# First scores ahead of the setup work: a two-network graph attention kernel on one Trainium2 core

## The reference, cut to what matters

```python
def first_network(x, adj):                 # three layers, 16 graphs
    mask = adj + eye > 0
    for l in range(3):
        si, sj = x @ attn_w[l, :256], x @ attn_w[l, 256:]
        s = leaky(si[:, :, None] + sj[:, None, :] + attn_b[l], 0.2)
        attn = softmax(where(mask, s, -inf))
        h = layernorm(x + attn @ x) * g1[l] + beta1[l]
        x = layernorm(h + gelu(h @ W1[l] + b1[l]) @ W2[l] + b2[l]) * g2[l] + beta2[l]
    return x
def second_network(x, A):
    xp = x @ W_proj                        # 8 heads of 32 columns
    a_src, a_dst = per head: xp . W_att[:, :32], xp . W_att[:, 32:]
    s = leaky(a_src[i] + a_dst[j] + b_att, 0.2)
    return relu(softmax(where(A > 0, s, -1e30)) @ xp)
x = norm(x + first_network(x, adj))
x = norm(x + second_network(x, adj))
```

## Time and profile before

| | us |
|---|---|
| median of 3 executions | 2322.6 (2321.7 to 2323.94) |
| the profiled execution, its own time | 2323.47 |
| its span in the trace | 2321.7 |
| PE busy | 2213.5 (95%) |
| DVE busy | 1809.9 (78%) |
| ACT busy | 1684.1 (73%) |
| POOL busy | 201.1 (9%) |

### The profile page before, as it was taken

One profiled execution on the slowest core, in us unless ns is written; L12 is line 12 of the kernel. 1 busy time (PEld: TensorE's weight loads), 2 busy tenths in 40 slices (PEclk: granted clock), 3 DMA queues, 4 the chain that ended last, 5 costly groups with the idle time before them and its releaser, 6 DMA issues.

```text
span 2321.7 us, 32320 instructions
## 1 busy us (share of the span) xinstructions
PE 2213.5 (95%) x10501; PEld 1560.0 (67%) x10501; DVE 1809.9 (78%) x5722; ACT 1684.1 (73%) x3243; POOL 201.1 (9%) x200
## 2 busy tenths in 40 slices
PE   3999999999999999999999999999999999999976
PEld 2676767766776677677677667766776776777643
DVE  5457587779788787887788787887878878766778
ACT  2433468776778778787787777787778877888796
POOL 0010110000100010001100001000010011001100
PEclk9999999999999999999999999999999999999978
DMA  6011024343163232532443421632316323200111
GB/s 219 11 37 55 10 96 135 93 150 101 46 197 109 76 127 54 188 105 63 133 130 103 153 90 58 188 104 89 124 47 199 97 65 104 69 19 19 37 42 37
DMA packets 115874, 219.30 MB, mean 94 GB/s; under 512 B 7768, under 2 KB 57212, under 8 KB 110332
## 3 DMA queue, kind: packets, MB, share of 16 engines
q1 hardware_dynamic: 115708, 217.24, 29.8%
HBM read 164.52 MB, written 52.69 MB: 94 GB/s over the span
## 4 chain that ended last, share of the span: by engine, by line
PE 75%; DVE 16%; ACT 5%; issue 3%; POOL 1%; DMA 0%; SPq 0%; DVEq 0%; POOLq 0%; ACTq 0%
PE ffn L1240 21%; PE av L1157 14%; PE ffn L1229 11%; PE av L1229 11%; PE pT L1140 8%; PE av L1181 4%; DVE prob L777 2%; DVE prob L768 2%; PE av L1216 2%; ACT xs L555 1%; DVE lone L729 1%; POOL rstd L469 1%; PE trow L1119 1%; DVE xs L903 1%; DVE stats L716 1%
## 5 line engine op out<-in xcount | busy, mean ns | idle before, releaser
L1240 PE MATMUL ffn<-w_sb,G 128*128 128x256 f32 x3072 | 741.1, 381 | 0.0
L1240 PEld LDWEIGHTS ffn<-w_sb,G 128*128 128x128 f32 x3072 | 561.3, 191 | 90.3 <-issue 24.3
L777 DVE CUSTOM_DVE_ANT_0 prob<-trow,mask 128x512 f32<-128x512 f32 x676 | 439.3, 686 | 34.3 <-PE trow L1119 19.4
L1229 PE MATMUL ffn<-hT,w_sb 128*128 128x512 f32 x768 | 355.0, 595 | 1.1 <-ACT hT L534 1.1
L1140 PEld LDWEIGHTS pT<-ident,prob 128*128 128x128 f32 x2032 | 255.9, 143 | 148.0 <-issue 101.6
L1229 PE MATMUL av<-hT,w_sb 128*128 128x512 f32 x768 | 353.5, 593 | 0.0
L469 POOL TENSOR_TENSOR rstd<-veps,mhalf 128x4 f32<-128x4 f32 x127 | 167.2, 1317 | 2082.9 <-DVE veps L712 2082.9
L515 ACT ACTIVATE prob<-prob,s 128x512 f32<-128x512 f32 x484 | 331.5, 716 | 2.4 <-DVE nm L784 1.8
L1140 PE MATMUL pT<-ident,prob 128*128 128x128 f32 x2032 | 312.1, 278 | 20.0 <-DVE prob L840 7.6
L521 ACT ACTIVATE prob<-prob,nm 128x512 f32<-128x512 f32 x448 | 317.7, 712 | 0.0
L1157 PE MATMUL av<-xs,prob 128*128 128x257 f32 x1024 | 244.3, 380 | 3.9 <-ACT prob L526 3.9
(11 more groups left out here) (154 smaller groups left out, 2727.2 us busy)
## 6 DMA issues: line engine op xcount, KB each, us to landing
w_sb<-in_L_gnn_W SPq DMA_DIRECT2D x48, 1024.0 KB, 8.4
blocks_dram<-blocks SPq DMA_DIRECT2D x168, 256.0 KB, 4.2
prob<-blocks_dram SPq DMA_DIRECT2D x42, 1024.0 KB, 4.8
trow<-rows_dram SPq DMA_DIRECT2D x127, 256.0 KB, 3.2
adj_sb<-in_adj SPq DMA_DIRECT2D x16, 1024.0 KB, 7.0
xin<-in_x SPq DMA_DIRECT2D x16, 512.0 KB, 6.3
x0r<-in_x SPq DMA_DIRECT2D x16, 512.0 KB, 5.8
out<-o SPq DMA_DIRECT2D x15, 512.0 KB, 3.3
```

Source lines behind the costliest of these rows:

```text
L777: return v.tensor_tensor_reduce(out=out_[:, t, :], in0=targets, in1=mask[:, t, :], scale=1.0, scalar=LEAST, op0=ALU.add, op1=ALU.max, accu ...
L1229: last = te.matmul(ff1[f % len(ff1)][:], w1_sb[:, g // 2 % STAGES, dt, f * P:(f + 1) * P], hT[:, dt, :], start=dt == 0, stop=dt == DT - 1)
L1240: last = te.matmul(ffn[part][:, at:at + D], G[:, f, t * P:(t + 1) * P], w2_sb[:, g // 2 % STAGES, f, :], start=f == 0, stop=f == FT - 1)
```

## The change

`aw_row` and `ab_row` count on a semaphore of their own, `s_aw`, and the others, now 11, stay on `s_const`. DVE waits for the two alone ahead of `scores(0, 0)`. The wait for `s_const` and the addition of the bias stand behind `first_exponents`, ahead of the first `attended`. The products and sums for the projection's attention columns become a function, `weights_with_attention`, called in slot 1 between the two halves of `fed_forward`. On PE the wait for `s_const` and the transpose of the columns stand behind the attention of unit 0, on ACT the copy to `cols` behind `probabilities`. `s_setup` is gone. No transfer is moved on SP, and no instruction that computes is added or taken away.

```diff
--- before.py
+++ after.py
@@ -44,7 +44,7 @@
 LAST_HEADS = (PAIRS - 1) * 2 * HEADS
 ATTENDED, RESIDUAL, FED, LAST = range(4)
 COLS = LAYERS * (2 * DT + FT)
-CONSTS = 13
+CONSTS = 11
 
 
 class Counts:
@@ -247,7 +247,7 @@
         def sem(name):
             return ctx.enter_context(nc.semaphore(name))
 
-        s_const, s_wts, s_setup, s_init, s_idn = sem("const"), [sem("wts0"), sem("wts1")], sem("setup"), sem("init"), sem("idn")
+        s_const, s_aw, s_wts, s_init, s_idn = sem("const"), sem("aw"), [sem("wts0"), sem("wts1")], sem("init"), sem("idn")
         s_colT, s_cols = sem("colT"), sem("cols")
 
         s_xin = [sem("xin0"), sem("xin1")]
@@ -341,8 +341,9 @@
 
             load_adj(0)
             load_x(0)
-            bcast(aw_row[:].rearrange("p l a d -> p (l a d)"), attn_w.rearrange("l d -> (l d)"))
-            bcast(ab_row[:], attn_b)
+            sp.dma_start(aw_row[:].rearrange("p l a d -> p (l a d)"),
+                         attn_w.rearrange("l d -> (l d)").partition_broadcast(P)).then_inc(s_aw, 16)
+            sp.dma_start(ab_row[:], attn_b.partition_broadcast(P)).then_inc(s_aw, 16)
             bcast(g1_row[:].rearrange("p l d -> p (l d)"), g1.rearrange("l d -> (l d)"))
             bcast(bias_row[:].rearrange("p l d -> p (l d)"), beta1.rearrange("l d -> (l d)"))
             bcast(g2_row[:].rearrange("p l d -> p (l d)"), g2.rearrange("l d -> (l d)"))
@@ -499,9 +500,6 @@
         @block.scalar
         def _(act):
             c = Counts()
-            act.wait_ge(s_colT, 1)
-            nc.scalar.copy(cols[:], ffn[0][:, 0:COLS]).then_inc(s_cols, 1)
-            act.wait_ge(s_cols, 1)
             def score0(u, t):
                 if t == 0:
                     act.wait_ge(s_nm0, u + 1)
@@ -580,6 +578,9 @@
                 score0(0, t)
             for t in range(T):
                 probabilities(t)
+            act.wait_ge(s_colT, 1)
+            nc.scalar.copy(cols[:], ffn[0][:, 0:COLS]).then_inc(s_cols, 1)
+            act.wait_ge(s_cols, 1)
             normalise(ATTENDED, y_att, xs[0], s_hn)
             for dt in range(DT):
                 transposed(dt, 0)
@@ -982,29 +983,32 @@
                                            ALU.subtract, ALU.mult)
                 last.then_inc(s_out, 1)
 
+            def weights_with_attention():
+
+                watt = watt_in.rearrange("p (h a k) -> p h a k", h=HEADS, a=2)
+                products = prod.rearrange("p (h k) -> p h k", h=HEADS)
+                for dt in range(DT):
+                    for a in range(2):
+                        v.tensor_tensor(products, wp_sb[:, dt, 0:D].rearrange("p (h k) -> p h k", h=HEADS),
+                                        watt[:, :, a, :], ALU.mult).then_inc(s_dch, 1)
+                        dve.wait_ge(s_dch, c("dch"))
+                        v.tensor_reduce(wp_sb[:, dt, D + a * HEADS:D + (a + 1) * HEADS], products, AX.X, ALU.add).then_inc(s_dch, 1)
+                        dve.wait_ge(s_dch, c("dch"))
+
             for b in xin + xs:
                 last = v.memset(b[:, :, D:D + 1], 1.0)
             last.then_inc(s_init, 1)
             dve.wait_ge(s_idn, 3)
             make_masks(0)
-            dve.wait_ge(s_const, 16 * CONSTS)
-            watt = watt_in.rearrange("p (h a k) -> p h a k", h=HEADS, a=2)
-            products = prod.rearrange("p (h k) -> p h k", h=HEADS)
-            for dt in range(DT):
-                for a in range(2):
-                    v.tensor_tensor(products, wp_sb[:, dt, 0:D].rearrange("p (h k) -> p h k", h=HEADS),
-                                    watt[:, :, a, :], ALU.mult).then_inc(s_dch, 1)
-                    dve.wait_ge(s_dch, c("dch"))
-                    v.tensor_reduce(wp_sb[:, dt, D + a * HEADS:D + (a + 1) * HEADS], products, AX.X, ALU.add).then_inc(s_dch, 1)
-                    dve.wait_ge(s_dch, c("dch"))
-            flat = bias_row[:].rearrange("p l d -> p (l d)")
-            v.tensor_tensor(flat, flat, b2_in, ALU.add).then_inc(s_dch, 1)
-            dve.wait_ge(s_dch, c("dch"))
-            dve.sem_inc(s_setup, 1)
+            dve.wait_ge(s_aw, 32)
             scores(0, 0)
             first_targets(0)
             for t in range(T):
                 first_exponents(t)
+            dve.wait_ge(s_const, 16 * CONSTS)
+            flat = bias_row[:].rearrange("p l d -> p (l d)")
+            v.tensor_tensor(flat, flat, b2_in, ALU.add).then_inc(s_dch, 1)
+            dve.wait_ge(s_dch, c("dch"))
             attention(0, 0)
             make_masks(1)
 
@@ -1051,6 +1055,8 @@
                 if done is not None:
                     graph_out()
                 fed_forward(s, 0)
+                if g == 1:
+                    weights_with_attention()
                 if k == 2:
                     keep_masks(0)
                 if k == 3 and p < PAIRS - 1:
@@ -1288,14 +1294,13 @@
                 attend(s, l, u, 3)
 
             pe.wait_ge(s_idn, 3)
+            first_target_row()
+            attention(0, 0, 0, lambda i: None)
             pe.wait_ge(s_const, 16 * CONSTS)
             te.transpose(ffn[0][:, 0:COLS], col_rows, ident[0:COLS, 0:COLS]).then_inc(s_colT, 1)
-            first_target_row()
-            attention(0, 0, 0, lambda i: None)
             for dt in range(DT):
                 transpose_state(0, dt)
             pe.wait_ge(s_cols, 1)
-            pe.wait_ge(s_setup, 1)
 
             for g in range(UNITS - 1):
                 (_, s, l), (_, s2, l2) = unit_of(g), unit_of(g + 1)
```

## The result

| | before | after |
|---|---|---|
| median, us | 2323.57 (2321.7 to 2324.5, 5 runs) | 2311.43 (2311.13 to 2312.53, 5 runs) |
| profiled execution, own time | 2323.47 | 2312.53 |
| its span | 2321.7 | 2310.8 |

The ratio is 0.995, interval 0.9936 to 0.9965: faster by 0.5%. The busy times did not move (TensorE 2213.5 and 2213.7, DVE 1809.9 and 1809.3), so what went was idle time of TensorE ahead of its work. The median before is of five executions here; the three that the forecast started from had 2322.6. In medians the gain is 12.1 us, between the two profiled executions 10.9.

What follows compares the result with a forecast made beforehand. TensorE is busy for 95% of the span, so only its late start, hanging on DVE's wait for W_proj ahead of the first scores, was left; -11.11 + 0.3 = -10.8 from the median 2322.6 gave 2311.8 us, range 2308 to 2317.

Steps and rivals of the forecast that it cites:

- What bounds the start: Ahead of slot 0's first product: all hangs on DVE's first scores, so a microsecond taken there is one off the end.
- 11.11 us at the scores: DVE's first scores start at 13.04 in place of 24.15, 11.11 us earlier, with 0.22 for the new wait.
- Vectors landed by 10.0, at 11 if an engine lags: `aw_row` and `ab_row`, landing estimated by counting small packets, arrive 2 to 3 us ahead of the need at 13.04.
- What is late next: Graph 1's adjacency lands at 34.3, 0.6 us before its masks start; up to 9.81 us of lateness covered; cost nothing.
- Bias, columns on TensorE and copy at nothing: Bias (0.96 us) behind the exponents, columns' transpose and ACT copy behind attention: hidden by longer waits, cost nothing.
- Columns in slot 1: +0.3 through POOL: Eight DVE instructions (3.65 us) between fed_forward's halves: free on DVE, but delay POOL's rstd and shift; cost 0.3 us.
- The clock: TensorE's clock falls in idle stretches; half a stretch more or less makes up to 1.7 us; likeliest 2309 to 2315.
- falls at other pauses: Clock behind TensorE's L1216 pauses: the shift loses both falls (2308.4) or gives two more (2315.2); chance 0.09.
- the slower case: Most L1216 pauses tip into clock falls, 1.7 us each; loss over 0.2% from ten more (2328.8); chance 0.02.
- Late vectors: At the start, `aw_row` and `ab_row` land with the last constants at 19.3; time 2318.3, no measurable change; chance 0.05.
- POOL held through all eight: Slot 1: the eight column instructions hold POOL throughout, +3.4 us in place of +0.3, clock falls 1.7; 2316.6; chance 0.05.
- More falls: Clock behind L1216 pauses: two more falls give 2315.2 (either direction chance 0.09), most pauses tipping a slowdown (chance 0.02).

Runs made afterwards that it cites:

- e9: Changed kernel with graph 0's masks split, row maximum and diagonal products moved behind the exponents, ahead of the bias; 2310.67 us.
- e12: Changed kernel unaltered, run again in the same call as three other runs to measure scatter; 2311.91 us.
- e3: Changed kernel with the transfers of `aw_row` and `ab_row` issued behind W_proj instead of behind the features; 2316.92 us.
- e6: Changed kernel with an added DVE copy of the masks (128 x 2048 bf16) in slot 1 ahead of the columns; 2311.51 us.
- e5: Changed kernel with an added, unused DVE product of two SBUF tensors (128 x 768 float32) in slot 1 ahead of the columns; 2313.29 us.
- e2: Changed kernel with TensorE's wait for all constants and its transpose of the columns back in front of the first target row; 2316.65 us.
- e7: Changed kernel with plus_bias (L884, 1.22 us on DVE) moved ahead of the attended tiles in every slot; 2301.53 us.
- e8: Changed kernel with plus_bias (L884) moved ahead of the attended tiles in slots 0 to 5 alone; 2304.32 us.
- e10: Changed kernel with plus_bias (L884) moved behind the first attended tile in every slot; 2290.81 us, ratio 0.986.

## Why the prediction was right, point by point

- **What bounds the start.** Right. The gain was idle time and work ahead of the scores, and the rest followed. Forecast 2311.8, measured 2311.43. That this is within 0.4 is in part luck: the forecast gain was 10.8 from a median of 2322.6, the measured one 12.1 from 2323.57. Between the profiled executions it was 10.9, by terms that cancel: 0.4 more than forecast at the scores and 0.3 less cost in slot 1, against 0.6 lost between the scores and the end.
- **11.11 us at the scores.** 11.54 in the profiled pair. 0.24 of the difference is the adjacency, which let DVE begin the masks at 6.23 in place of 6.47, which no edit accounts for. The rest is the new wait: I gave it 0.22, and between L746's end and the scores were 0.04.
- **Vectors landed by 10.0, at 11 if an engine lags.** `aw_row` 9.4, `ab_row` 10.3. In e9 and e12 `ab_row` landed at 9.9 and 10.0. Counting small packets gave the landing to 0.3 us where no row timed it. e3 and e9 show the other side: where the vectors are later, or DVE earlier, they are in the line.
- **What is late next.** Right: graph 1's adjacency was in time at 34.87, and where it was late (e9) the 9 us of cover held.
- **Bias, columns on TensorE and copy at nothing.** Right. With the bias in front of it DVE still idles 3.02 ahead of the first attended tile (3.45 before), and TensorE 6.51 ahead of the transposes (6.63 before).
- **Columns in slot 1: +0.3 through POOL.** This term was wrong in its mechanism, and small. The step that failed is "copies and two-operand work hold POOL": I read rstd's stretch by the copy in slot 2 as valid for a product as well. The runs show two things in its place. A copy holds even the end of a POOL instruction under way (e6), a product only one that comes during it (e5). In the changed kernel the product came when rstd was nearly through, and shift came 0.11 us ahead of the product's end and took its usual 0.20. The term was 0.
- **Trainium skill, "SBUF — State Buffer", section on the shared port.** It says that whoever starts first keeps the ports for the whole instruction. That rstd would hold off the first product is not what happened: L992 started at 116.08 during rstd, as long as ever (0.41), and the measurement decides. The section confines the exclusion by two SBUF inputs to a GpSimd instruction that reads SBUF. shift does, and with e5, shift held for 0.5 us, this agrees. rstd reads SBUF too, so this does not explain why L992 was not held; that stays open.
- **The clock.** The width was right in kind: one fall came (1.5 us, slot 3), one went (1.7, slot 6), and little of it is left in the end. The count behind it was wrong. The 26 waits and 53.7 us of the earlier trace rows are those of a line, matmuls and weight loads together. TensorE's own list, before the change, has half as many (us, times, longest):

```profile
PE av L1216 <- ACT xs L555: 24.2, 13, 6.6
```

  One of the 13 is the start and six are 1.09 us long. So two of six long pauses in the slots were followed by a fall, and not two of 26. That speaks for more than the 0.09 given to falls at other pauses, and ten more, on which the slower case stood, would have had to come behind the pauses of 1.09 as well.
- **The rivals.** Late vectors: shown not to hold here, and real when forced (5.5 us). POOL held through all eight: no. More falls: two behind the pauses of the slots before, two after. The gain of 0.5% is clear of no change by its interval.

## What to carry to other kernels

A semaphore that counts a dozen loads makes its first reader wait for the last of them; give what the first step reads its own, and then move every engine's wait in that line, since one left in front (TensorE's, e2) took back 5.2 of the 12.1 us. Where nobody waits for a transfer its landing can still be had, by counting packets in windows. Look also at what runs on DVE while a short POOL step that TensorE waits for is under way: in the first slots each pause of TensorE got 0.9 us shorter. And look at what stands in DVE's own line ahead of the scores that TensorE waits for. Moving one 1.2 us product to a place where DVE idles did both here and was worth 20.6 us, nearly twice the change; of the 22.3 between the profiles 6.3 were such pauses. When a view gives a count of waits, check that it is the waits of one engine.

## What was not expected of the hardware

- rstd, 128x4 on POOL, takes 1.01 us beside DVE work that reads PSUM (e7), 1.91 when an SBUF product is under way as it comes, and 2.41 when a bf16 copy comes upon its end (e6). A product that starts 0.22 us ahead of its end does not lengthen it. Beside L778 it takes 1.38, and beside L729, which has one SBUF input, 1.92 (shift: 1.23 in place of 0.20, e9): two inputs are not needed to hold POOL.
- The clock did not fall behind a pause of 2.13 us (e6), fell behind one of 2.38 in e12 and not behind one of 2.47 in the same run, and behind the 1.97 of slot 6 fell before the change, in e8 and in e12, and not in the changed kernel's first profile. Behind pauses of up to 1.21 us it did not fall in e7 and e10. Pause length alone does not decide it, and what does stays open.
